# Expert rows added into two running sums in DRAM by scattering DMAs that wait for each other

## What is computed

```python
glogits = h2 @ gate_w + gate_b
topv, topi = jax.lax.top_k(glogits, TOPK)          # TOPK = 4
gw = jax.nn.softmax(topv, axis=-1)
combine = jnp.zeros((N, E), x.dtype).at[jnp.arange(N)[:, None], topi].add(gw)
def body(acc, we):
    wu, wd, ce = we
    ug = h2 @ wu
    u, g = (ug[:, :DFF], ug[:, DFF:])
    return (acc + ce[:, None] * (jax.nn.silu(g) * u @ wd), None)
y2, _ = jax.lax.scan(body, jnp.zeros_like(h2), (W_up, W_down, combine.T))
return x + y2.reshape(Bx, Tx, Dx)
```

## Time and profile before

| what | value |
|---|---|
| time, median of 3 runs | 1331.48 us (1330.04 to 1337.93) |
| span of the profiled execution | 1334.7 us |
| busy share PE / PEld / DVE / ACT / POOL | 82% / 55% / 64% / 47% / 36% |
| DMA traffic | 57.68 MB |
| `layers` | until about 990 us |
| routing plan, zeroing of pads | about 990 to 1017 us |
| `experts`, first tile transposed to last scatter issued | 1017 to 1295 us |
| `combine` | 1301 us to the end |

### The profile page before, as it was taken

One profiled execution on the slowest core, in us unless ns is written; L12 is line 12 of the kernel. 1 busy time (PEld: TensorE's weight loads), 2 busy tenths in 40 slices (PEclk: granted clock), 3 DMA queues, 4 the chain that ended last, 5 costly groups with the idle time before them and its releaser, 6 DMA issues. The chain is left out here.

```text
span 1334.7 us, 22974 instructions
## 1 busy us (share of the span) xinstructions
PE 1096.2 (82%) x6360; PEld 733.2 (55%) x6361; DVE 852.9 (64%) x3025; ACT 629.8 (47%) x2211; POOL 486.0 (36%) x644
## 2 busy tenths in 40 slices
PE   6799999999989989998999999998833676676720
PEld 3345666666656656665666666555523665565620
DVE  5238787978869777886978879778731223223307
ACT  1016565565646646564665655656602333333310
POOL 3111214244233323423243243343250565656550
PEclk7659999999999999999999999999966988888765
DMA  7500000000000000000000000000023322323219
GB/s 217 167 0 1 2 1 18 1 18 12 8 18 0 17 1 17 15 3 18 0 17 10 10 18 1 18 18 5 14 65 93 88 78 72 93 80 84 72 40 315
DMA packets 65511, 57.68 MB, mean 43 GB/s; under 512 B 14961, under 2 KB 54802, under 8 KB 65426
## 3 DMA queue, kind: packets, MB, share of 16 engines
q1 hardware_dynamic: 49554, 33.81, 9.3%
q0 software_dynamic: 9216, 19.68, 4.5%
q10 hardware_dynamic: 6656, 3.25, 0.9%
HBM read 30.34 MB, written 26.35 MB: 42 GB/s over the span
## 5 line engine op out<-in xcount | busy, mean ns | idle before, releaser
L1096 POOL TENSOR_TENSOR l_t_cos<-l_t_cos,l_t_sin 128x512 f32<-128x512 f32 (+1 forms) x96 | 104.2, 1085 | 459.6 <-DVE l_t_sin L797 459.6
L961 ACT ACTIVATE l_prob<-l_score,l_nm 128x256 f32<-128x256 f32 (+1 forms) x512 | 213.2, 439 | 3.9 <-DVE l_nm L665 3.7
L1302 POOL DMA_INDIRECT expert_out<-e_yo,e_dest x160 | 153.2, 957 | 141.5 <-ACT e_yo L1428 95.2
L972 ACT COPY l_probT<-l_turned 128x512 f32<-128x512 f32 x192 | 112.9, 588 | 148.8 <-PE l_turned L366 142.2
L658 DVE TENSOR_REDUCE l_mx<-l_score 128x2 f32<-128x512 f32 (+1 forms) x192 | 131.9, 687 | 67.8 <-PE l_score L350 48.3
L366 PE MATMUL l_turned<-ident_sb,l_prob 128*128 128x128 f32 x768 | 123.6, 284 | 29.7 <-DVE l_prob L647 29.1
L94 POOL DMA_INDIRECT expert_rows<-h,slot x128 | 126.6, 989 | 43.1 <-issue 41.3
L647 DVE TENSOR_SCALAR l_prob<-l_prob,l_rec 128x256 f32<-128x256 f32 (+1 forms) x512 | 136.6, 322 | 6.8
L350 PE MATMUL l_score<-l_kpad,l_qT 128*128 128x512 f32 x256 | 134.3, 607 | 0.0
L382 PE MATMUL l_turned<-l_probT,l_vv 128*64 128x128 f32 x1536 | 126.3, 285 | 4.4 <-ACT l_probT L972 2.6
L382 PEld LDWEIGHTS l_turned<-l_probT,l_vv 128*64 128x64 f32 x1536 | 79.9, 136 | 68.1 <-ACT l_probT L972 40.9
(11 more groups left out here) (218 smaller groups left out, 2061.8 us busy)
## 6 DMA issues: line engine op xcount, KB each, us to landing
e_xt<-expert_rows SPq DMA_DIRECT2D x160, 70.0 KB
c_rows<-expert_out SPq DMA_DIRECT2D x16, 512.0 KB, 5.8
wup_sb<-in_wup SPq DMA_DIRECT2D x1, 4096.0 KB, 17.1
expert_rows<-zeros SPq DMA_DIRECT2D x48, 70.0 KB, 2.2
expert_out<-e_yo,e_dest POOLq DMA_INDIRECT x160
expert_rows<-h,slot POOLq DMA_INDIRECT x128
out_x<-c_res ACTq DMA_DIRECT2D x16, 128.0 KB, 5.7
expert_rows<-zeros ACTq DMA_DIRECT2D x16, 70.0 KB
```

Of the source, the lines that this page charges most:

```text
L961: ins = A_.activation(prob[:, b, cols], score[u % 3][:, cols], ACT.Exp, bias=nm[:, b, j:j + 1], scale=0.125, accum_out=sums[:, b, j:j + 1])
L972: A_.copy(probT[:, u % 2, :], turned[u % 2][:]).then_inc(s["probT"], 1)
L1096: g.tensor_tensor(t_cos[:, 0:w], t_cos[:, 0:w], t_sin[:, 0:w], ALU.add).then_inc(s["added"], 1)
L1302: g_.indirect_dma_start(m["ys"], bass.IndirectOffsetOnAxis(ap=dest[:, q, j:j + 1], axis=0), yo[:, q % 2, j, :], None).then_inc(sent[q % 2] ...
```

## The change

`ys` no longer has a row for every product. It holds two running sums, each of `SUM_ROWS` = 128 + 4096 rows (128 rows for padding, then one for each token). The scatter gets `compute_op=ALU.add`: the DMA adds its 512-byte rows to what lies in DRAM. Tiles 0 and 2 of a group go to the first sum, tiles 1 and 3 to the second (`sum_off`). Two scatters into one sum must not overlap, so POOL waits before each scatter for the landing of the one two tiles before it, in place of issuing them back to back. There are four `sent` semaphores, one for each place in the group, and POOL's loop is written out for the 40 groups.

The sums need a start value. SP stores zeros to the second sum and to the padding rows (34 stores of 64 KB), between the zeros of the tail and the three bias transfers. ACT's queue stores all of `x` (2 MB, one DMA) as the start of the first sum at the beginning of `experts`. The token order within `ys` is changed, so that a partition's 32 rows lie together; `pick_row` is computed by DVE in `constants()` from `iota_e` and `row_32`.

`combine` reads two rows for each token instead of four (8 rounds, each of two loads of 256 KB) and needs one DVE addition for each round; `x` is already in the first sum.

```diff
+SUM_ROWS = P + SEQS * TOK
-        m["ys"] = nc.dram_tensor("expert_out", [SPARE + SEQS * TOK * TOPK, D], F32, kind="Internal").ap()
+        m["ys"] = nc.dram_tensor("expert_out", [2 * SUM_ROWS, D], F32, kind="Internal").ap()
...
                 sp.dma_start(m["xs"][row:row + P, :], m["zeros"][:]).then_inc(m["tail_zeroed"], 16)
+
+            sp.dma_start(m["ys"][0:P, :], m["zeros"][:, 0:D]).then_inc(m["sums_zeroed"], 16)
+            for j in range(TILES + 1):
+                row = SUM_ROWS + j * P
+                sp.dma_start(m["ys"][row:row + P, :], m["zeros"][:, 0:D]).then_inc(m["sums_zeroed"], 16)
 
             sp.wait_ge(s["part"], 5)
...
+                V.tensor_scalar(m["row_32"][:], m["tile_id"][:, 0:1], float(TILES), float(P), ALU.mult, ALU.add) \
+                    .then_inc(s["part"], 1)
+                v.wait_ge(s["part"], 6)
...
+                V.tensor_scalar(m["pick_row"][:], m["iota_e"][:][:, :, None].broadcast_to([P, TILES, TOPK]),
+                                m["row_32"][:], None, ALU.add)
...
-            with pool.Fori(0, GROUPS // 4) as i:
-                for q in range(4):
-                    hold(pool, s["y"], i * 4 + (q + 1), s["held"])
-                    for j in range(GROUP):
-                        g_.indirect_dma_start(m["ys"], bass.IndirectOffsetOnAxis(ap=dest[:, q, j:j + 1], axis=0),
-                                              yo[:, q % 2, j, :], None).then_inc(sent[q % 2], 16)
+            def scatter(g, q):
+                pool.wait_ge(s["y"], g + 1)
+                for j in range(GROUP):
+
+
+                    if j >= 2:
+                        pool.wait_ge(sent[j - 2], g * 16 + 16)
+                    elif g > 0:
+                        pool.wait_ge(sent[j + 2], g * 16)
+                    g_.indirect_dma_start(m["ys"], bass.IndirectOffsetOnAxis(ap=dest[:, q, j:j + 1], axis=0),
+                                          yo[:, q % 2, j, :], None, compute_op=ALU.add).then_inc(sent[j], 16)
+
+            pool.wait_ge(m["sums_zeroed"], (TILES + 2) * 16)
+            pool.wait_ge(s["based"], 16)
+            for g in range(GROUPS):
+                scatter(g, g % 4)
...
-                    v.wait_ge(sent[q % 2], g * 32 - (q % 2 + 2) * 32)
+                    for j in range(GROUP):
+                        v.wait_ge(sent[j], g * 16 - 3 * 16)
...
-                V.tensor_tensor(dest[:, q], mine[:, q, :, 0], m["row_id"][:, bass.ds(g * GROUP, GROUP)], ALU.max) \
-                    .then_inc(s["dest"], 1)
+                V.scalar_tensor_tensor(out=dest[:, q], in0=mine[:, q, :, 0], scalar=m["tile_id"][:, 0:1],
+                                       in1=m["sum_off"][:], op0=ALU.max, op1=ALU.add).then_inc(s["dest"], 1)
...
             act_.wait_ge(s["counted"], 1)
+            act_.dma_start(m["ys"][P:SUM_ROWS, :].rearrange("(p t) d -> p t d", p=P), m["x"][:]).then_inc(s["based"], 16)
             zero_pads(act_, 1, s["padded_b"])
...
-                        act_.wait_ge(sent[b], h * 32 - b * 32)
+                        for j in range(GROUP):
+                            act_.wait_ge(sent[j], h * 16 - 16)
...
-    BUFS, LOADS = 4, 2
+    BUFS, LOADS = 4, 4
...
-                sp.dma_start(rows[:, i % BUFS], source(i)).then_inc(loaded[i % BUFS], 16)
+                    sp.wait_ge(summed, i - BUFS + 1)
+                for half in range(2):
+                    sp.dma_start(rows[:, i % BUFS, half], source(i, half)).then_inc(loaded[i % BUFS], 16)
...
-                V.tensor_tensor(res[:, b], one[:, b], x[:, i * LOADS:(i + 1) * LOADS, :], ALU.add) \
-                    .then_inc(summed, 1)
+                V.tensor_tensor(res[:, b], rows[:, b, 0], rows[:, b, 1], ALU.add).then_inc(summed, 1)
```

More of the change, by code:

```diff
@@ L144, in program @@
         m["zeros"] = sb("zeros", [P, WIDE])
+        m["row_32"] = sb("row_32", [P, 1])
+        m["sum_off"] = sb("sum_off", [P, GROUP])
+        m["sums_zeroed"] = ctx.enter_context(nc.semaphore("sums_zeroed"))
         prepare(m)
@@ L1219, in experts @@
              ("cnt_ps counted padded_a padded_b step placed rows_ps planned xT_ps xT up_ps act hid hidT_ps hidT y_ps y "
-              "eq pick mine dest held sent_a sent_b in_a in_b in_c in_d").split()}
+              "eq pick mine dest held sent_a sent_b sent_c sent_d in_a in_b in_c in_d based").split()}
         arrived = [s[n] for n in ("in_a", "in_b", "in_c", "in_d")]
-        sent = [s["sent_a"], s["sent_b"]]
+        sent = [s[n] for n in ("sent_a", "sent_b", "sent_c", "sent_d")]
         block = ctx.enter_context(nc.Block())
@@ L1296, in _ @@
                 send_pick(m, (SEQS - 1) % 2, c)
[L1298 to L1305 removed]
+            def scatter(g, q):
[12 more added lines that the diff above has]
+            for j in range(GROUP):
+                pool.wait_ge(sent[j], GROUPS * 16)
         @block.vector
@@ L1494, in sb @@
             return ctx.enter_context(nc.sbuf_tensor("c_" + name, shape, dt))
-        rows = sb("rows", [P, BUFS, LOADS, TOPK, D])
-        two, one = sb("two", [P, BUFS, LOADS, 2, D]), sb("one", [P, BUFS, LOADS, D])
+        rows = sb("rows", [P, BUFS, 2, LOADS, D])
         res = sb("res", [P, BUFS, LOADS, D])
@@ L1500, in combine, with source @@
         written = [ctx.enter_context(nc.semaphore(f"c_written{b}")) for b in range(BUFS)]
-        halved, added, summed = (ctx.enter_context(nc.semaphore("c_" + n)) for n in ("halved", "added", "summed"))
+        summed = ctx.enter_context(nc.semaphore("c_summed"))
         block = ctx.enter_context(nc.Block())
         N = TILES // LOADS
-        def source(i):
-            return m["ys"][SPARE + i * LOADS * P * TOPK:SPARE + (i + 1) * LOADS * P * TOPK, :] \
-                .rearrange("(t p k) d -> p t k d", p=P, k=TOPK)
+        def source(i, half):
+            first = half * SUM_ROWS + P
+            return m["ys"][first:first + SEQS * TOK, :].rearrange("(p t) d -> p t d", p=P)[:, i * LOADS:(i + 1) * LOADS, :]
         @block.sync
@@ L1520, in _ @@
                 b = i % BUFS
-                v.wait_ge(loaded[b], (i // BUFS + 1) * 16)
-                V.tensor_tensor(two[:, b], rows[:, b, :, 0:2, :], rows[:, b, :, 2:4, :], ALU.add) \
-                    .then_inc(halved, 1)
-                v.wait_ge(halved, i + 1)
-                V.tensor_tensor(one[:, b], two[:, b, :, 0, :], two[:, b, :, 1, :], ALU.add).then_inc(added, 1)
-                v.wait_ge(added, i + 1)
+                v.wait_ge(loaded[b], (i // BUFS + 1) * 32)
                 if i >= BUFS:
                     v.wait_ge(written[b], (i // BUFS) * 16)
-                V.tensor_tensor(res[:, b], one[:, b], x[:, i * LOADS:(i + 1) * LOADS, :], ALU.add) \
-                    .then_inc(summed, 1)
+                V.tensor_tensor(res[:, b], rows[:, b, 0], rows[:, b, 1], ALU.add).then_inc(summed, 1)
         @block.scalar
```

9 lines of the change are left out of this document (5 added, 4 removed).

## The result

The changed kernel takes 1378.19 us (median, 1376.07 to 1381.24), the kernel before beside it 1334.7 us (median, now of four runs; the first three had 1331.48): a ratio of 1.0324 [1.0287, 1.0361]. It is slower. The profiled execution has a span of 1374.0 us, 39.3 more than the span of before, which is 1334.7 us as well.

What follows compares the result with a forecast made beforehand. No engine was full in the experts stretch; POOL's scatters had the steady rhythm. 1334.7 + 52.8 + 0.9 + 16.2 - 11.9 = 1392.7 us profiled, less 3.2 for the median: 1389.5, given as 1390 us, range 1330 to 1460.

Steps and rivals of the forecast that it cites:

- The chain of scatters: Experts stage: each scatter waits for the landing two before, so 159 steps take 315.6 us instead of 262.8, +52.8 us.
- the forecast link of 3.97 us: Experts stage, one scatter's start to that of the one two later: 2.29 landing, 0.78 release to start, 0.9 addition.
- The 0.78 us from release to start: POOL in the experts stage: time from a wait's release to the scatter's start, claimed in every link, 0.78 us.
- The landing: Experts stage: the addition's read of DRAM lengthens start to landing, 2.29 us for a plain scatter, by 0.9 us.
- The zeros: Kernel start, SP's queue: 34 more stores ahead of the bias transfers, 0.475 us each, delay all behind them, +16.2 us.
- DVE's two instructions: New instructions in constants(), claimed to run long before 55 us, ahead of the idle stretch, and cost 0.
- The 2 MB store: ACT's queue, start of experts: pads' zeros behind it could be late; taken as 0, up to 6 us without cover.
- Combining: End of kernel, paced by the DMA engines: reads fall from 8.39 to 4.19 MB, -11.9 us.
- Rival A: Experts stage: the addition costs next to nothing, link 3.07 us or less, kernel faster at 1317 us; chance 0.09.
- Rival D: Experts stage: waits are free, at most 1.65 us a scatter, 1336 us; chance 0.13 together with A's edge.
- Rival B: Experts stage: addition dear through a read wholly before the write or longer descriptors, link 4.87 us, 1462 us; chance 0.23 with beyond.
- Rival C: Kernel start: the zeros cost nothing, PE's wait being filled by something else, 1373 us; chance 0.05.

Runs made afterwards that it cites:

- e3: e1 with four sums instead of two, each scatter waiting only for the one four tiles before, 66 more zero stores: 1352.04 us, ratio 1.0145.
- e1: Changed kernel with its 34 zero stores for the sums issued behind the three bias transfers instead of in front: 1365.38 us, ratio 1.0249.
- e4: e1 with the 2 MB store behind the pads' zeros and, at a group's first scatter, the wait for y ahead of the landing's: 1344.53 us, ratio 1.0584.
- b3: b1 with the bias transfers ahead of SP's 32 stores of zeros: 1286.76 us, ratio 1.0139.
- e6: The same program as e1, run again beside the changed kernel: 1363.66 us, ratio 1.0222.
- e5: The changed kernel itself run again, no edit, beside the kernel before: 1380.86 us, ratio 1.0342.
- e2: Changed kernel without the addition in the scatter (plain writes), all waits, zeros and short combining kept: 1320.87 us, ratio 0.9897.
- b1: Kernel before, plain scatters, with the change's waits for the landing two tiles before and POOL's loop written out: 1325.71 us, ratio 0.9938.
- b5: The same program as b1, run again beside the kernel before: 1324.48 us, ratio 0.993.
- b2: Kernel before with POOL's loop over the groups written out and no added waits: 1270.34 us, ratio 1.0005.

## Why the prediction came out as it did

Forecast 1390, measured 1378.19 us. The direction held, and so did the size of the main term; what makes up that term was wrong, and the last sum came nearer than its parts. The sum for the profiled execution was 1392.7 us and the span is 1374.0, 18.7 less: 7.8 are the chain of scatters (+52.8 forecast, +45.0 measured), 10.9 the stretch up to the first scatter (16.2 forecast, 5.3 in this trace), and the rest cancels. The median hides 7.4 of the 18.7 us, and that is luck: I took it 3.2 us below the span, as before, and it is 4.2 above it.

- **The chain of scatters: +52.8 forecast, +45.0 measured.** The sum was near, its makeup was not. I put the addition at 0.9 us in the link from landing to landing and left POOL's instruction at its 0.96 us, with the remark that longer descriptors were inside the bounds. The instruction became 1.554 us, and with the 0.30 behind it (1.86) it is the bound of this stage: e3, nearly without waits, has 1.861 a step, the changed kernel 1.936. The waits that I thought set the pace add 11.9 us (14.5 between e1 and e3, on one chip). That the forecast link of 3.97 us is near the measured 3.87 (two steps of 1.936) is luck: 0.6 us of POOL's instruction was left out, and a 0.78 us that is mostly absent was put in. The sign that I had named for being wrong here, a duration of a scatter on POOL far from 0.96 us, is there, and the one for being right, that POOL's longest waits are for landings, is not.
- **The 0.78 us from release to start, in each link: false for most.** I read it off the first scatter of a group, where POOL's wait is for `yo`. The timeline of the changed kernel shows what a wait for a landing costs:

```profile
1046.44 1.55 POOL L1325 DMA_INDIRECT expert_out<-e_yo,e_dest  x1 [0.30 <-issue]
1048.30 1.55 POOL L1325 DMA_INDIRECT expert_out<-e_yo,e_dest  x1 [0.30 <-issue]
1050.21 1.55 POOL L1325 DMA_INDIRECT expert_out<-e_yo,e_dest  x1 [0.36 <-DMA expert_out<-e_yo,e_dest]
1052.73 1.55 POOL L1325 DMA_INDIRECT expert_out<-e_yo,e_dest  x1 [0.97 <-DMA expert_out<-e_yo,e_dest]
1053.49 1.14 ACT L1459 ACTIVATE e_yo<-e_p_y,e_mine 128x128 f32<-128x128 f32 x4 [5.28 <-DMA expert_out<-e_yo,e_dest]
```

  Within this group the gap grows only from 0.30 to 0.36 us; only at 1052.73, the first of the next group, with its two waits, is it 0.97. The link 1046.44 to 1050.21 is 3.77 us, where I had 3.97, and 3.72 of it are POOL's own two steps of 1.86.
- **The landing: +0.9 forecast, +1.0 measured.** The group's last scatter starts at 1050.21 and ACT, which waits for it, runs at 1053.49: 3.28 us instead of 2.29. The time from a scatter's start to its landing is 3.3 us in the middle in e4 and 2.3 in b3, which has no addition. But 0.60 of the 0.99 is POOL's longer instruction; what lies behind it grew by 0.4. The 0.8 us that the Trainium skill gives for the shortest round trip to HBM (DMA: Bandwidth & Descriptors, section on latency and other measured facts), taken as the extra, would have made the sum 8 us less and so nearer. That is an estimate from the page; measured, the extra behind POOL's part is half of it, so the figure was near the whole only by the same accident as mine, and no run here shows that access by itself.
- **The zeros: +16.2 forecast, +16.3 at the place, 17.2 in the time** (e6 beside e5).
- **What I did not foresee: 11 us given back in the layers.** I had costed DVE's two instructions at 0, since they run in idle time. They did, but they moved what stands behind them, and 10.0 of the 11 us lie at the three returns of the loop. This took the result away from the forecast, not towards it: without it the result would by this estimate have been about 1388, but only because the chain's 7.8 us too much stand against the 7.4 of the median. What arrives at the first scatter isn't constant either, 5.3 us later than before in this trace, 9.5 and 11.0 in the two pairs that ran on one chip each (e2 and b1, e5 and b5).
- **The 2 MB store: 0 forecast, about +2.4.** The delay is 2.9 us at the end of the layers (`l_t_cos` starts at 912.79 and not at 909.86 us) and 5.3 at the first scatter. The row of the first tile loads is at 1018.75 us against 1013.46, behind the pads that the store goes ahead of. Of the 6 us that it could cost without its cover, part was paid. No run takes this store alone away from its place on one chip, so the 2.4 is read from two traces. It is not clear of the spread: from the last `l_t_cos` to the first scatter e1 takes 108.4 us and e6, the same program on another chip, 111.7. On the chip of e4, with the store behind the pads, 1.3 us are left against b2 and b3.
- **Combining: -11.9 forecast, -12.1 measured.** The DMA engines set its length as before: over the whole stretch their busy share is 0.89 (0.90 before) at 293 GB/s (311 before). DVE's 8 additions take 5.5 us, less than the third of its 24 that I wrote.
- **Rival A** asked for an addition that costs nothing. e2, without the addition, is that case: 1320.87 us, where I had 1317 with the full 16.2 us of the zeros in it. Its lower bound for the chain, 244.1 us, was too low by 8.8: the waits for `yo` don't all go. **Rival D**, the waits free: for plain scatters it holds where bursts have holes (e2, b1, b5) and not on the chip of b3; for those that add it falls by 14.5 us (e1 against e3). **Rival B** was right in that POOL's instruction grew, and wrong in how far: its step would be over 2.3 us. **Rival C** fell with e6.

## What to carry to other kernels

Before a plain transfer is changed into one that does something with its data, ask what the issuing engine pays for it, not only what the memory does: here the pace is set by 0.6 us more in an instruction of POOL, and halving the rows of combining gives 12 us back for 45. Stores that nobody waits for yet belong behind the transfers that somebody does (17 us here, 9 in the kernel before). An edit ahead of a loop can change the stalls inside it, so a delay should be followed along the trace from its place to the end before it is added up.

## What the runs showed of the hardware beyond what I expected

- A scatter of 128 rows of 512 bytes that adds takes 1.554 us on POOL, a plain one 0.957, and the queue counts 27136 packets for the same 19.68 MB that were 9216 before; the share of the DMA engines' time is 10.1% instead of 4.5%. With 288 scatters on the queue, all plain before and 160 of them adding after, that is 32 packets for a plain one and, if the 128 plain ones left have as many, 144 for one that adds. Before and after:

```profile
q0 software_dynamic: 9216, 19.68, 4.5%
```

```profile
q0 software_dynamic: 27136, 19.68, 10.1%
```

- The kernel before took 1269 us on one chip and 1332 to 1348 on the others; 57 of the 65 us between 1269 and 1335 lie in the scatters (a step of 1.294 us, read from b2, or 1.653). The change with waits around such bursts came out on the other side of 1 there (0.994 and 0.993 against 1.014, the last with SP's order changed as well).
- A stall of DVE of 5.3 us at a loop's return had the clock at 0.50 for about 3 us behind it, one of 2.9 us did not; two instructions far ahead of the loop make the difference.
